# A stage of its own for the triangular inverses is folded into the stage before it, and the gate's shared product is made once per tile

## The reference, cut to what matters

```python
q, k, v = silu(conv(hs @ Wq)), silu(conv(hs @ Wk)), silu(conv(hs @ Wv))
beta = sigmoid(hs @ Wb)                               # 4 heads of 64
q, k = q / sqrt(sum(q*q) + 1e-12), k / sqrt(sum(k*k) + 1e-12)
v, kb = v * beta, k * beta                            # chunks of c = 32 tokens
A = where(strictly_lower, kb @ k.T, 0)                # 32 x 32 for each chunk and head
inv = inverse(eye + A); u = inv @ v; w = inv @ kb
for each chunk: u_i = u - w @ S; o = q @ S + where(lower, q @ k.T, 0) @ u_i; S += k.T @ u_i
short, long = causal convolutions of v, 5 and 64 taps
stats = [mean, var, mean|x|, l2 norm] of short, long, delta (= o) and v, for each head   # 16 numbers
hgate = gelu(concat(hs, stats) @ mlp_w1 + mlp_b1)     # for each head; hs is the same for all four
probs = softmax((hgate @ mlp_w2 + mlp_b2) / temp) * 0.84 + floor
o = probs mix of short, long, delta and v, + sigmoid(c) * short
out = (o * rsqrt(mean(o*o) + 1e-5) * rms_w) @ Wo
```

## Time and profile before

| | value |
|---|---|
| device time, median of 3 runs | 5963.18 us (5955.74 to 5968.25) |
| span of the profiled execution | 5957.4 us, 119901 instructions |
| PE busy / PE weight loads | 5355.5 us (90%) / 4244.1 us |
| VectorE busy | 4264.6 us (72%) |
| ScalarE busy | 2668.3 us (45%) |
| GpSimd busy | 2612.1 us (44%) |
| DMA | 357.50 MB, mean 60 GB/s |

### The profile page before, as it was taken

One profiled execution on the slowest core, in us unless ns is written; L12 is line 12 of the kernel. 1 busy time (PEld: TensorE's weight loads), 2 busy tenths in 40 slices (PEclk: granted clock), 3 DMA queues, 4 the chain that ended last, 5 costly groups with the idle time before them and its releaser, 6 DMA issues. The chain is left out here.

```text
span 5957.4 us, 119901 instructions
## 1 busy us (share of the span) xinstructions
PE 5355.5 (90%) x42776; PEld 4244.1 (71%) x42776; DVE 4264.6 (72%) x13841; ACT 2668.3 (45%) x6214; POOL 2612.1 (44%) x3780
## 2 busy tenths in 40 slices
PE   6999999999999999988966636999999999999987
PEld 5888888888888888867944424777777777777755
DVE  4777777777777777762238875888888888888871
ACT  2555555555555555542133322444444444444441
POOL 1222222222222222222277742666666666666660
PEclk8999999999999999998955556999999999999998
DMA  1011011011011011006755542222222222222211
GB/s 41 28 36 37 29 35 36 29 34 37 29 35 36 29 35 36 29 29 134 190 149 141 141 108 57 61 62 62 62 61 62 61 60 59 60 62 61 62 35 45
DMA packets 599702, 357.50 MB, mean 60 GB/s; under 512 B 336400, under 2 KB 589136, under 8 KB 599120
## 3 DMA queue, kind: packets, MB, share of 16 engines
q1 hardware_dynamic: 528656, 314.18, 18.9%
q10 hardware_dynamic: 65664, 16.78, 1.2%
q0 software_dynamic: 4800, 18.88, 1.1%
HBM read 212.59 MB, written 137.10 MB: 59 GB/s over the span
## 5 line engine op out<-in xcount | busy, mean ns | idle before, releaser
L526 POOL TENSOR_TENSOR a_shift<-a_mean_var,a_eps 128x2 f32<-128x2 f32 x256 | 71.3, 279 | 1834.9 <-DVE a_mean_var L736 1834.9
L2136 PE MATMUL c_bank<-c_xT,c_gate 128*128 128x512 f32 x1024 | 503.0, 614 | 0.7 <-ACT c_statsT L1889 0.7
L750 DVE SCALAR_TENSOR_TENSOR a_cv<-a_raw,a_taps,a_cv 128x256 f32<-128x256 f32 x1152 | 461.9, 479 | 19.5 <-ACT a_cv L628 10.0
L820 PE MATMUL a_bank<-a_w,a_hidden 128*128 128x256 f32 x2048 | 459.1, 382 | 0.9 <-ACT a_hidden L613 0.9
L918 PE MATMUL a_bank<-a_turned,a_w 128*128 128x256 f32 x2048 | 453.0, 379 | 1.1 <-ACT a_turned L574 1.1
L820 PEld LDWEIGHTS a_bank<-a_w,a_hidden 128*128 128x128 f32 x2048 | 383.8, 190 | 71.8 <-issue 20.6
L918 PEld LDWEIGHTS a_bank<-a_turned,a_w 128*128 128x128 f32 x2048 | 384.1, 190 | 51.2 <-ACT a_turned L574 1.6
L1786 POOL TENSOR_TENSOR c_expd<-c_e,c_logit 128x16 f32<-128x16 f32 x128 | 371.7, 2904 | 50.7 <-DVE c_logit L1972 37.9
L1772 POOL TENSOR_TENSOR c_stats<-c_l2sq,half 128x16 f32<-128x16 f32 x128 | 373.4, 2917 | 15.1 <-DVE c_l2sq L1961 15.1
L2140 PEld LDWEIGHTS c_bank<-c_statsT,c_gate_stats 128*128 128x128 f32 x2048 | 270.0, 192 | 124.9 <-issue 124.9
L1356 POOL TENSOR_TENSOR i_coef<-i_base,i_exponent 128x12 f32<-128x12 f32 x128 | 298.9, 2335 | 71.6 <-issue 52.8
(11 more groups left out here) (295 smaller groups left out, 14140.7 us busy)
## 6 DMA issues: line engine op xcount, KB each, us to landing
a_x<-in_x SPq DMA_DIRECT2D x64, 256.0 KB, 3.3
scratch_xb<-a_xb SPq DMA_DIRECT2D x64, 256.0 KB, 2.1
scratch_q<-a_qkv_rows SPq DMA_DIRECT2D x64, 256.0 KB, 2.2
scratch_k<-a_qkv_rows SPq DMA_DIRECT2D x64, 256.0 KB, 2.7
scratch_v<-a_qkv_rows SPq DMA_DIRECT2D x64, 256.0 KB, 3.0
b_window<-scratch_v SPq DMA_DIRECT2D x8, 2048.0 KB, 22.1
scratch_long<-b_out ACTq DMA_DIRECT2D x8, 2048.0 KB, 24.4
scratch_short<-b_out POOLq DMA_DIRECT2D x8, 2048.0 KB, 18.0
```

Source lines behind the costliest of these rows:

```text
L750: ins = dve.scalar_tensor_tensor(cv[s][:, n, c], raw[s][:, n, c, j:j + TOK], taps[:, n, c, j:j + 1], cv[s][:, n, c], ALU.mult, ALU.add)
L820: ins = pe.matmul(dst[:, t * D:(t + 1) * D], src[s][:, c, tile_cols(t)], weight[:, c], start=(c == 0), stop=(c == chunks - 1))
L2136: pe.matmul(dst[:].rearrange("p (h t) -> p h t", h=H), gate1[:, c, cols], xT[sl][:, c:c + 1].broadcast_to([P, H, P]), start=(c == 0), stop ...
```

## The change

**Stage A takes the inverse stage over.** New steps stand behind those that were there: `beta` after `qkv1` (four products with 4 columns, from xT of xb that is in SBUF; ScalarE copies -x out, and the sigmoid is formed on GpSimd as (1 + e^-x) to the power -0.5, its root being wanted); `squares` after `qkvT`, of q and k while they are in SBUF; `powers` (GpSimd, 24 numbers of a token, and the scaled keys); `kT` (four transposes), `gram` (32 products), `keep` (VectorE, with the negative strictly lower mask), and the stores. After the last step of a sequence `gather` loads its 128 triangles twice (as A and as the start of T) and the inversion follows in four pieces (`inverse0` to `inverse3`) for each later step. There are 16 inversions of one set of 128, where there were 8 of two sets. All shares of A are new, and so is the order of its steps. To make room, `phik_rows`, `phiq_own`, `v_own`, `resid` and `xa` have one slot instead of two, with waits for the step before. `phase_i` goes.

**Stage C's gate.** A new step `base` makes xb's product once, for both halves in one bank: four products with 128 columns. ScalarE writes it (`seed`) into two banks that are kept out of the rotation (`PRE`, the last two; the other jobs share six), twice 512 columns, broadcast over the heads. The statistics are laid out anew, so that heads 0 and 1 lie in rows 0 to 63 and heads 2 and 3 in rows 64 to 127 of `statsT`; a column of ones carries the bias `gate_b1`. The eight statistics products have 64 rows each and alternate between the two row groups and the two banks, adding to what ScalarE wrote. The gelu loses its bias operand. The share of `l2` goes from 2.7 to 1.7 and `base` has 1.0; the other shares and `DEPTH` stay.

The diff, cut to its core:

```diff
@@ class PsumPlan
-    def __init__(self, order, jobs_of, base, iterations):
+    def __init__(self, order, jobs_of, base, iterations, held=()):
+        shared = [b for b in range(BANKS) if b not in held]
...
-            b = n % BANKS
+            b = shared[n % len(shared)]
@@ phase_a
-    DEPTH = 4.779
+    PERIOD = 10.437
...
-              ("lnB_stats", 1.69), ("lnB", 1.72), ("xbT", 3.97), ("qkv1", 3.91), ("conv", 1.64), ("qkvT", 0.01)]
+              ("lnB_stats", 2.29), ("lnB", 4.0), ("xbT", 1.39), ("qkv1", 0.11), ("beta", 4.14), ("conv", 1.31),
+              ("qkvT", 1.43), ("squares", 2.59), ("powers", 1.48), ("kT", 0.02), ("gram", 1.54), ("keep", 2.06),
+              ("gather", 33.88), ("inverse0", 2.71), ("inverse1", 2.74), ("inverse2", 2.76), ("inverse3", 0.01)]
...
-        phik_rows = slots("phik_rows", [P, T, D], 2)
+        phik_rows = slots("phik_rows", [P, T, D], 1)
...
+            def powers(i, s):
+                pool.wait_ge(S["ssq_ready"], seq(i, s))
+                in_sbuf(pool, i, s, "beta")
...
+                link(pool.tensor_tensor(beta, e_base[:], beta, ALU.pow))
+                link(pool.tensor_tensor(beta, beta, one_base[:], ALU.add))
+                link(pool.tensor_tensor(coef[s][:], base[s][:], powers_half[:], ALU.pow))
...
+            def invert(piece):
+                def stage(i, s):
...
+                        link(dve.tensor_tensor(part, A_[:, j:j + 1, below_j].broadcast_to(shape),
+                                               T_[:, 0:j, j:j + 1].broadcast_to(shape), ALU.mult))
+                        rest = T_[:, 0:j, below_j]
+                        ins = dve.tensor_tensor(rest, rest, part, ALU.add)
...
-def phase_i(nc, w, k, scratch, batches, banks):
...
@@ phase_c
+    PRE = [BANKS - C + m for m in range(C)]
+    plan = PsumPlan(order, jobs_of, banks.count, TILES, held=PRE)
...
-        stats = slots("stats", [P, 2, H, SRC, NSTAT], 2)
+        stats = slots("stats", [P, H, 2, SRC, NSTAT], 2)
...
+            def seed(i, s):
+                src_ = full(act, i, s, "base")
+                for m in range(C):
...
+                    ins = act.activation(psum[PRE[m]][:].rearrange("p (c h t) -> p c h t", c=C, h=2),
+                                         src_[:, 0:C * P].rearrange("p (c t) -> p c t", c=C)[:, :, None, :].broadcast_to([P, C, 2, P]), ACT.Copy)
+                    ins.then_inc(N["pre_seeded"], 1)
...
+            def gate_base(i, s):
+                dst = open_bank(i, s, "base", "xT")
+                for m in range(C):
+                    cols = slice(m * P, (m + 1) * P)
+                    for c in range(C):
+                        ins = pe.matmul(dst[:, cols], gate1[:, c, cols], xT[s % SLOTS][:, c], start=(c == 0),
+                                        stop=(c == C - 1))
...
             def gate(i, s):
...
-                    for c in range(C):
-                        pe.matmul(dst[:].rearrange("p (h t) -> p h t", h=H), gate1[:, c, cols],
-                                  xT[sl][:, c:c + 1].broadcast_to([P, H, P]), start=(c == 0), stop=False,
-                                  skip_group_check=True)
...
+                pe.wait_ge(N["pre_seeded"], C * seq(i, s))
                 for m in range(C):
+                    for n in range(2):
+                        for g in range(PAIRS):
+                            rows = slice(g * DH, (g + 1) * DH)
+                            at = (2 * m + n) * P
+                            ins = pe.matmul(psum[PRE[g]][:, at:at + P], gate1_stats[rows, 2 * g + n, m * P:(m + 1) * P],
+                                            statsT[sl][rows, :], start=False, stop=True, skip_group_check=True)
```

More of the change, by code:

```diff
@@ L30 @@
 BANKS = 8
+CUT = 32
 def pipelined(shares, steps, depth):
@@ L295, in phase_a @@
         "xdT": ["xdT"], "ffn": ["ffn"], "xbT": ["xbT"], "qkv1": ["raw0", "raw1", "raw2"],
-        "qkvT": ["qkvT0", "qkvT1", "qkvT2"],
+        "beta": ["beta"], "qkvT": ["qkvT0", "qkvT1", "qkvT2"], "kT": ["kT"], "gram": ["G0", "G1"],
     }
     plan = PsumPlan(order, jobs_of, banks.count, batches)
+    HEADS, HEAD = 4, D // 4
+    PAIRS = HEADS // 2
+    BLOCKS = P // CUT
+    SIDE = CUT * CUT
+    PIECES = 4
+    columns_of = [[0]] + [[2 * m - 1, 2 * m] for m in range(1, STEPS * PIECES)]
     x_v = x.rearrange("(n t p) d -> n p t d", t=T, p=P)
+    coef_v = scratch["coef"].rearrange("(n t p) c -> n p t c", t=T, p=P)
+    below_v = scratch["below"].rearrange("n (h p j) -> n p h j", h=HEADS, j=CUT)
+    sets_v = {n: scratch[n].rearrange("(i n) (q m) -> i (n q) m", n=STEPS * T, m=SIDE) for n in ("below", "inverse")}
     out_v = {n: scratch[n].rearrange("(n t p) d -> n p t d", t=T, p=P) for n in ("xb", "q", "k", "v")}
@@ L370, in phase_a @@
         shift = slots("shift", [P, 4, T], 4)
+        base = slots("base", [P, T, 3, HEADS], 2)
+        coef = slots("coef", [P, T, 3, HEADS], 2)
+        powers_half = sb("powers_half", [P, T, 3, HEADS])
+        e_base = sb("e_base", [P, T, HEADS])
+        one_base = sb("one_base", [P, T, HEADS])
+        kn = slots("kn", [P, T, D], 1)
+        kT = slots("kT", [P, PAIRS, TOK], 1)
+        below = slots("below", [P, T, HEADS, CUT], 2)
+        drop_block = sb("drop_block", [P, CUT])
+        A_sets = [sb(f"A{n}", [P, CUT, CUT]) for n in range(2)]
+        T_sets = [sb(f"T{n}", [P, CUT, CUT]) for n in range(2)]
+        product = sb("product", [P, SIDE // 4])
         rden = slots("rden", [P, T, H], 2)
@@ L429, in _ @@
             def _(dve):
+                for b in range(BLOCKS):
+                    rows = slice(b * CUT, (b + 1) * CUT)
+                    dve.tensor_tensor(drop_block[rows], k["ident"][rows, rows], k["keep_causal"][rows, rows], ALU.subtract)
                 dve.wait_ge(landed, 16 * len(loads))
@@ L577, in turned_norm, with evacuate @@
                 return stage
-            def evacuate(job, dst):
+            def evacuate(job, dst, taken_by=None):
                 def stage(i, s):
+                    if taken_by is not None and not_first(i, s, 1):
+                        computed(act, *back(i, s, 1), taken_by)
                     src = full(act, i, s, job)
@@ L761, in _ @@
             stages = {
+                "squares": sums, "keep": keep,
                 "ln1_stats": norm_stats(0, x_sb, S["ln1_var"], True),
@@ L1646, in _ @@
                 pool.memset(floor[:, :, 0:2], FLOOR)
+                for ones in stats[0:2]:
+                    pool.memset(ones[:, :, 1, 0, 0:1], 1.0)
                 later = keep[:, 0].rearrange("p (b n) -> p b n", n=CUT)
@@ L2169, in _ @@
             stages = {"turn_x": turn_x, "turn_qk": turn_qk, "gram": gram, "kS": k_state, "o": o_of, "dS": new_state,
-                      "statsT": turn_stats, "pre": gate, "logits": logits, "oT": turn_o, "Wo": project}
+                      "statsT": turn_stats, "base": gate_base, "pre": gate, "logits": logits, "oT": turn_o, "Wo": project}
+            for m in range(C):
+                pe.matmul(psum[PRE[m]][:], ident[:], gate1_stats[:, 0:2].rearrange("p h d -> p (h d)"), start=True,
+                          stop=True).then_inc(N["pre_opened"], 1)
             for b in range(BLOCKS):
```

486 lines of the change are left out of this document (194 added, 292 removed).

## The result

The changed kernel takes 6148.31 us (median of 4 runs, 6138.62 to 6155.40) against 5964.44 us before: the ratio is 1.031 (95% interval 1.029 to 1.032), 3.1% slower. 6080 us was forecast, with a range of 5500 to 6290.

What follows compares the result with a forecast made beforehand. TensorE was taken to pace stage A, and a TensorE-VectorE ring stage C. -601 (inverse stage) + 147 (A, work) + 109 (A, clock) + 50 (tail) + 415 (C) = +120 us: 6080 us, range 5500 to 6290.

Steps and rivals of the forecast that it cites:

- Inverse stage, -601: Between stages B and C: removing the block from 3002.9 to 3604.3 saves 601 us, its bytes hidden in stage A.
- Work moved into A, +147: Stage A: new TensorE products and transposes plus 0.5 us idle add 2.3 us to each of 64 steps, +147 us.
- A's clock, +109: Stage A: thin products behind qkv1 cause one half-clock stretch a step, +109 us (bounds 0 and +190).
- Slots cut to one, at nothing: Stage A: buffers cut from two slots to one wait only for work ordered earlier, costing nothing.
- Tail of A, +50: End of stage A: the last store, gather and dependent inversion leave TensorE idle, about +50 us.
- The ring and the gap: Stage C: TensorE and VectorE alternate through carry2; 3.3 us cut from the gate saves 0.25 us, the rest becomes idle before solve2.
- VectorE's half: Stage C: VectorE's stretch from the new state's products to the next carry2, 8.3 us, said not to shrink.
- Six banks, at nothing: Stage C: rotating jobs over six PSUM banks meets no late reader, so it costs nothing.
- The clock in C, +415: Stage C: lost wide products and idle time bring half clock; steps average 19.8 us, +415 us (bounds -32 and +710).
- TensorE's half: Stage C: TensorE's stretch from solve2 to the new state's products, 7.9 us at full clock, 13.7 us at half.
- the share of slow steps: Stage C: six steps in ten at 22.1 us, the other four at 16.3 us.
- Sum: Whole kernel: all savings and costs together give +120 us, for a time of 6080 us.

Runs made afterwards that it cites:

- the row groups alone: Changed kernel, but TensorE makes xb's product for all heads, without base or ScalarE's write; statistics products stay in two row groups: 5677.95 us, ratio 0.952.
- The thin fill: Changed kernel plus 19 useless products of 32 rows, 32 weight columns and 64 moving columns behind stage C's gate each step: 6024.71 us.
- The order with Wo moved: Changed kernel with xb's product by TensorE, Wo before solve2, oT and turn_x behind dS, GpSimd's order kept, A's bank skip moved: 6298.50 us, ratio 1.057.

## Why the prediction was right, and where it was off

- **Inverse stage, -601:** -601.4 measured. Right, and the bytes hid.
- **Work moved into A, +147, and A's clock, +109:** together xn's transposes end 277.6 us later (2841.2 against 2563.6), 256 were forecast. The work is the smaller term: 42.2 us for the commonest step is about 2 us over the mean before, where 2.3 were taken. The idle time at gram and den was right in kind (0.75 and 1.06 us). The rest, some 2.3 us a step, is half-clock stretches and one wait that the prediction lacks: it did not look at the banks of A, where 148 jobs over eight banks skip four at each turn of the sequence. Its price is 3.64 us of waiting for each of 16 sequences, 58 us, and what the clock loses behind it.
- **Slots cut to one, at nothing:** no wait on them is among TensorE's in the table from 1000 to 2600 us.
- **Tail of A, +50:** 330.5 - 277.6 = 52.9 us. Right.
- **The ring and the gap:** right in each place named: TensorE stands still before solve2 for VectorE's carry2, VectorE's waits at carry1 and Wo are longer (2.67 and 1.52 us, 1.27 and 0.58 in the earlier trace rows), and at full clock a cut gate gains nothing (16.6 us with the row groups alone, 16.3 forecast). Wrong in one term: VectorE's half, 8.3 us, was said not to shrink, and it is 7.8 us, since its operations no longer meet GpSimd's.
- **Six banks, at nothing:** nearly. The prediction found no late reader, but 320 jobs over six banks skip two at the turn from lane 15 to lane 0, and solve2 then gets a bank in which gram's product lies. From 3400 to 5400 us TensorE waits for VectorE to read it, in all, times, longest:

```profile
PE c_bank L1998 <- DVE c_grams L1818: 13.0, 6, 3.5
```

That is some 17 us of the stage, an estimate from these 2000 us.
- **The clock in C, +415:** +449.1 measured. The mechanism was right and its picture was not: not six slow steps of 22.1 us in ten with four of 16.3 between them, but nearly every step with a stretch at half clock, most of them 20.2 us. The clock falls only some 2 us into TensorE's half, so that half is 12.4 us and not 13.7, and VectorE's is 7.8 and not 8.3; and the clock rises behind dS in these steps, though the gap follows each time. The average, 19.8 against 20.27, came near by luck: the share of slow steps, six in ten, was a choice with nothing measured behind it, too low, and the price of one was too high.
- **Sum:** +120 forecast, +179.5 in the spans, +184 in the medians: 34 us too little in C, 22 in A's steps, 3 in the tail, 1 in B and D.

The Trainium skill (TensorE: Matmul & The Clock Gate, Part 1) has idle gaps between bursts as what costs the clock. By that rule stage C goes slow in every step, and the trace agrees as to the steps (+449 us; the prediction priced it at +710). The thin fill does not agree: TensorE hardly stood still in front of solve2 and the clock was 0.79. The order with Wo moved, with 92% busy and 0.75, has a gap of 1.2 us a step and decides nothing.

Why the clock falls at carry3 and rises behind dS is only placed by the traces, not explained. That wide products in the gap in front of solve2 help was shown for this spot; which spot is the best was not tried.

## What to carry to other kernels

Wide products on TensorE may be what keeps its clock up for the thin ones: before they are taken out or moved, read what stands behind them and what the stretch costs at half clock, and try the saving with useless products in its place, once wide and once thin: the two runs tell the gap from the want of wide products. Draw the ring of the recurrence before costing a cut: what lies in the other engine's half paid nothing here. A change that alters the number or the order of the jobs in a rotation of banks, or the order on an in-order engine such as GpSimd, moves waits to places that it does not touch: read the table of waits after each such change, before the result is put down to what was meant to change.

## What the runs showed of the hardware that was not expected

Useless work made a kernel 7.4% faster. And VectorE's convolution in stage A got slower though its code is the same. The group on the page, before and after:

```profile
L750 DVE SCALAR_TENSOR_TENSOR a_cv<-a_raw,a_taps,a_cv 128x256 f32<-128x256 f32 x1152 | 461.9, 479 | 19.5 <-ACT a_cv L628 10.0
```
```profile
L878 DVE SCALAR_TENSOR_TENSOR a_cv<-a_raw,a_taps,a_cv 128x256 f32<-128x256 f32 x1152 | 566.9, 565 | 10.0 <-DVE a_scaled L810 9.9
```

Its shortest, median and longest time (ns) in the changed kernel, and the timelines of VectorE and GpSimd at one of them:

```profile
L878 DVE SCALAR_TENSOR_TENSOR a_cv<-a_raw,a_taps,a_cv x1152: 451/473/1497, 165.0 to 2988.2; 128x256 f32<-128x256 f32 x192
```
```profile
2652.89 0.80 DVE L878 SCALAR_TENSOR_TENSOR a_cv<-a_raw,a_taps,a_cv 128x256 f32<-128x256 f32 x1 [0.16 <-DVE a_scaled L810]
...
2652.15 1.27 POOL L605 TENSOR_TENSOR a_x<-a_x 128x512 f32<-128x512 f32 x1
2653.50 1.33 POOL L606 TENSOR_TENSOR a_x<-a_x,a_b 128x512 f32<-128x512 f32 x1
```

Its median is unchanged (479 ns before), but some take up to 1497 ns, 105 us more in all: the new order has put GpSimd's two additions of the residual beside two of them a step. All 124 that take over 520 ns overlap L606, and half of them L605 too. The Trainium skill (SBUF — State Buffer, "SBUF: two separate sides") has it that of a VectorE operation with two inputs in SBUF and a GpSimd operation that reads SBUF the one that starts first keeps the other out for its whole length. These rows agree, and so do those of the three small operations in stage C. Whether it cost time in stage A was not tested; in stage C it is 0.5 us of nearly every step at full clock.
